# Filter stage of a four-layer graph network: a new order of DVE and PE work, four gather buffers, laps of four turns

## The reference, cut to what matters

```python
Wf = ssp(ssp(edge_attr @ m1_W + m1_b) @ m2_W + m2_b)     # 50 -> 256 -> 256, for each edge
msg = h1[src] * Wf                                       # 256 values for each edge
agg = jax.ops.segment_sum(msg, dst, num_segments=n_nodes)
# ssp(x) = softplus(x) - log(2)
```

## Time and profile before

| What | us |
|---|---|
| Median of the runs | 6121.58 |
| Runs, lowest to highest (3) | 6119.18 to 6132.07 |
| Span of the profiled execution, first to last instruction | 6128.0 |
| Filter stage in it, from the first instruction to the end of the last add | 4328.8 to 5264.5 |

### The profile page before, as it was taken

The page is one execution under the profiler, slowest core; times in us unless marked ns, Lnnn a source line. Parts: engine busy times, 40 slices in busy tenths (PEclk is TensorE's granted clock), DMA queues, the critical chain, the costliest instruction groups (busy, mean ns, idle before and its releaser), DMA issues. The chain is left out here.

```text
span 6128.0 us, 77751 instructions
## 1 busy us (share of the span) xinstructions
PE 4062.0 (66%) x17164; PEld 2958.9 (48%) x17165; DVE 3143.4 (51%) x7175; ACT 1987.0 (32%) x4687; POOL 3556.1 (58%) x2851
## 2 busy tenths in 40 slices
PE   5599922596777769677677444445688888745553
PEld 5488811353555555355556333333455555533332
DVE  5577636522555542355554344445477777533334
ACT  0122200000665541266563122220477777400000
POOL 0244411277777725677773788865555555478884
PEclk9999966798887879788787655557799999866555
DMA  0000002234665534566552233333234343243332
GB/s 7 24 10 10 10 27 61 77 77 94 172 168 154 158 89 92 135 171 166 153 156 61 62 84 83 84 79 89 71 102 103 103 104 103 79 101 84 84 84 73
DMA packets 511546, 558.56 MB, mean 91 GB/s; under 512 B 302820, under 2 KB 394959, under 8 KB 511005
## 3 DMA queue, kind: packets, MB, share of 16 engines
q0 software_dynamic: 349600, 362.07, 24.5%
q1 hardware_dynamic: 158408, 187.29, 10.7%
q10 hardware_dynamic: 3250, 6.40, 0.4%
HBM read 460.45 MB, written 92.22 MB: 90 GB/s over the span
## 5 line engine op out<-in xcount | busy, mean ns | idle before, releaser
L1259 POOL DMA_INDIRECT sum_gx_sb<-scratch_xw,keep_k_row_step_sb x1272 | 1602.7, 1260 | 469.9 <-issue 351.3
L1372 PE MATMUL sum_a_ps<-sum_gx_sb,sum_sel_sb 125*125 125x258 f32 (+1 forms) x4320 | 1214.4, 445 | 539.5 <-ACT sum_gx_sb L1308 218.9
L1372 PEld LDWEIGHTS sum_a_ps<-sum_gx_sb,sum_sel_sb 125*125 125x125 f32 x4320 | 936.1, 242 | 732.2 <-issue 514.1
L1308 ACT ACTIVATE sum_gx_sb<-sum_gx_sb,sum_wt_sb 125x129 f32<-125x129 f32 x3312 | 981.8, 388 | 561.5 <-DVE sum_wt_sb L1501 527.2
L2473 POOL DMA_INDIRECT filter_gx_sb<-scratch_h,keep_k_src_step_sb x424 | 513.5, 1211 | 410.6 <-DVEq L2620 299.0
L1168 POOL DMA_INDIRECT scratch_grouped<-keep_k_value_sb,keep_k_place_sb x400 | 481.7, 1204 | 272.6 <-issue 137.1
L2917 POOL DMA_INDIRECT source_gx_sb<-scratch_h,source_grouped_sb x424 | 527.5, 1244 | 140.4 <-issue 117.5
L2929 PE MATMUL source_s_ps<-source_gx_sb,source_sel_sb 125*125 125x257 f32 x848 | 370.0, 612 | 310.8 <-DMA source_gx_sb<-scratch_h,source_grouped_sb 310.8
L2929 PEld LDWEIGHTS source_s_ps<-source_gx_sb,source_sel_sb 125*125 125x125 f32 x848 | 246.3, 304 | 434.5 <-issue 172.1
L2527 PE MATMUL filter_ps<-filter_m_sb,filter_h_sb 128*125 128x256 f32 x1728 | 403.9, 387 | 15.6 <-DVE filter_f_sb L2592 15.3
L2527 PEld LDWEIGHTS filter_ps<-filter_m_sb,filter_h_sb 128*125 128x125 f32 x1728 | 318.2, 189 | 141.9 <-issue 98.2
(11 more groups left out here) (513 smaller groups left out, 6861.5 us busy)
## 6 DMA issues: line engine op xcount, KB each, us to landing
scratch_hots<-sum_cuts_sb SPq DMA_DIRECT2D x108, 244.1 KB
filter_sel_sb<-scratch_hots SPq DMA_DIRECT2D x106, 244.1 KB
sum_gx_sb<-scratch_xw,keep_k_row_step_sb POOLq DMA_INDIRECT x1272
scratch_xw<-gate_xsb_sb SPq DMA_DIRECT2D x50, 253.9 KB
scratch_xw<-attend_xsb_sb SPq DMA_DIRECT2D x25, 507.8 KB
filter_ea_sb<-in_ea_t SPq DMA_DIRECT2D x436, 24.4 KB
filter_gx_sb<-scratch_h,keep_k_src_step_sb POOLq DMA_INDIRECT x424
source_gx_sb<-scratch_h,source_grouped_sb POOLq DMA_INDIRECT x424
```

The source lines that it names most:

```text
L1259: nc.gpsimd.indirect_dma_start(out=gx[:, q, j, :], out_offset=None, in_=table, in_offset=bass.IndirectOffsetOnAxis(ap=keep["row_step"][:, ...
L1308: last = nc.scalar.activation(here, here, ACT.Copy, scale=wt[q][:, h, j:j + 1])
L1372: last = mm(psa[b][0:P, half, 0:BF], sel[:, 0, p, j, :], gx[:, q, at, half * BF:(half + 1) * BF], **flags)
```

## The change

- DVE's order in a turn becomes: `make_f2` for turn r+2, `make_h1` for r+3, `products` (the second softplus and the product) for r+1, then `add` for r. The messages `ms` get two buffers, so that they are made one turn ahead of the sums.
- PE's order becomes `hidden` for r+4, the sums for r, `filters` for r+3.
- `node_tiles` is called once a turn for four tiles, behind the product and ahead of the wait for the sums. The drain between product and `ms_made` is gone; the product raises `ms_made` itself, and POOL waits for `ms_made` in place of `used`.
- `gx` has four buffers with a semaphore each; POOL no longer waits for the weights at the start.
- The loops of all engines hold four turns (a lap) in place of two. Turns that don't exist are left out (`runs`), so the surplus `hidden` and `filters` are gone.
- The start: `ea_free` is raised before the clearing of `agg`, not after it.
- Each group's four adds, each with its drain, are kept as they are.

```diff
-    gx = mem.sb("gx", [P, 2, HF, D])
+    LAP = 4
+    QUADS = STEPS // HF
+    LOOPS = (QUADS - 6) // LAP
+    gx = mem.sb("gx", [P, LAP, HF, D])
...
-    f2, lg2 = ([mem.sb(f"{n}{q}", [P, HF, D]) for q in range(2)] for n in ("f2", "lg2"))
-    ms = mem.sb("ms", [P, HF, D])
+    f2, lg2, ms = ([mem.sb(f"{n}{q}", [P, HF, D]) for q in range(2)] for n in ("f2", "lg2", "ms"))
...
+    def laps(engine, lap):
+        lap(-1, LAP)
+        with engine.Fori(0, LOOPS) as i:
+            lap(i, LAP)
+        for i in range(LOOPS, -(-QUADS // LAP)):
+            lap(i, min(LAP, QUADS - i * LAP))
...
-            pool.wait_ge(landed, 16 * 4)
             for step in range(STEPS):
-                j, q = step % HF, step // HF % 2
-                if j == 0:
-                    pool.wait_ge(used, step // HF + 1)
+                j, n = step % HF, step // HF
+                if j == 0 and n >= LAP:
+                    pool.wait_ge(ms_made, n - LAP + 1)
...
+            def lap(i, count):
+                for r in range(count):
+                    load(i, r + 5)
+                    load_hots(i, r + 2)
...
+            def lap(i, count):
+                for r in range(count):
+                    hidden(i, r + 4)
+                    if runs(i, r):
+                        sums(i, r)
+                    filters(i, r + 3)
...
+            def lap(i, count):
+                for r in range(count):
+                    parts = []
+                    if runs(i, r + 1):
+                        act.wait_ge(f2_made, i * LAP + r + 2)
+                        parts.append(filters[(r + 1) % 2])
+                    if runs(i, r + 3):
+                        act.wait_ge(hid, i * LAP + r + 4)
+                        parts.append(hidden[(r + 3) % 2])
+                    log(parts)
...
+            def products(i, r):
+                if runs(i, r):
+                    dve.wait_ge(log2_made, i * LAP + r + 1)
+                    vec.scalar_tensor_tensor(f2[r % 2][:], f2[r % 2][:], 0.0, lg2[r % 2][:], ALU.max, ALU.add)
+                    dve.drain()
+                    dve.wait_ge(x_in[r % LAP], i * (16 * HF) + (r // LAP + 1) * (16 * HF))
+                    vec.tensor_tensor(ms[r % 2][:], f2[r % 2][:], gx[:, r % LAP], ALU.mult).then_inc(ms_made, 1)
+
+            def add(i, r, tiles):
+                dve.wait_ge(summed, i * LAP + r + 1)
+                for j in range(HF):
+                    here = agg[:, bass.ds(tiles[j], 1), 0:D].rearrange("p o f -> p (o f)")
+                    vec.tensor_tensor(here, ps3[0:P, j, :], here, ALU.add)
+                    dve.drain()
+                dve.nop().then_inc(added, 1)
+
+            def lap(i, count):
+                for r in range(count):
+                    make_f2(i, r + 2)
+                    make_h1(i, r + 3)
+                    products(i, r + 1)
+                    if runs(i, r):
+                        add(i, r, node_tiles(nc, keep, (i * LAP + r) * HF, HF))
+                    else:
+                        dve.drain()
...
             vec.memset(half[:], 0.5)
+            dve.drain()
+            dve.nop().then_inc(ea_free, 1)
             for t in range(0, NT + 1, 13):
                 vec.memset(agg[:, t:t + 13, 0:D], 0.0)
             dve.drain()
-            for sem in (ea_free, added, used, used):
-                dve.nop().then_inc(sem, 1)
+            dve.nop().then_inc(added, 1)
```

More of the change, by code:

```diff
@@ L2452, in filter_sum, with runs, later @@
     lg1, h1 = ([mem.sb(f"{n}{q}", [128, 2, C4]) for q in range(2)] for n in ("lg1", "h1"))
-    f2, lg2 = ([mem.sb(f"{n}{q}", [P, HF, D]) for q in range(2)] for n in ("f2", "lg2"))
-    ms = mem.sb("ms", [P, HF, D])
+    f2, lg2, ms = ([mem.sb(f"{n}{q}", [P, HF, D]) for q in range(2)] for n in ("f2", "lg2", "ms"))
     sel = mem.sb("sel", [P, 2, HF, P])
     ps1, ps2, ps3 = [mem.ps(f"1{q}", [128, 2, 512]) for q in range(2)], mem.ps("2", [128, HF, D]), mem.ps("3", [128, HF, D])
-    (landed, used, ea_free, hid, log1_made, h1_made, filt, f2_made, log2_made, ms_made,
+    (landed, ea_free, hid, log1_made, h1_made, filt, f2_made, log2_made, ms_made,
      summed, added) = (mem.sem(n) for n in (
-         "landed", "used", "ea_free", "hid", "log1_made", "h1_made", "filt",
-         "f2_made", "log2_made", "ms_made", "summed", "added"))
-    x_in, e_in, hot_in = ([mem.sem(f"{n}{q}") for q in range(2)] for n in ("x", "e", "hot"))
+         "landed", "ea_free", "hid", "log1_made", "h1_made", "filt", "f2_made", "log2_made", "ms_made",
+         "summed", "added"))
+    x_in = [mem.sem(f"x{q}") for q in range(LAP)]
+    e_in, hot_in = ([mem.sem(f"{n}{q}") for q in range(2)] for n in ("e", "hot"))
     vec, mm = nc.vector, nc.tensor.matmul
-    TURNS, U2 = STEPS // (2 * HF), 2 * HF
+    def runs(i, r):
+        return not isinstance(i, int) or 0 <= LAP * i + r < QUADS
+    def later(i, r, first):
+        return not isinstance(i, int) or LAP * i + r >= first
+    def laps(engine, lap):
[4 more added lines that the diff above has]
+            lap(i, min(LAP, QUADS - i * LAP))
     with nc.Block() as block:
@@ L2482, in _ @@
             sp.dma_start(mb[:], dr["L2_gnn_m2_b"].partition_broadcast(P)).then_inc(landed, 16)
[L2484 to L2491, removed]
@@ L2493, in _, with load @@
-            sp.wait_ge(ea_free, 1)
[L2494 to L2505, removed]
+            def load(i, r):
+                if runs(i, r):
+                    if later(i, r, 2):
+                        sp.wait_ge(hid, i * LAP + r - 1)
+                    for j in range(HF):
+                        tile = sp.value_load(keep["etile"][0:1, bass.ds((i * LAP + r) * HF + j, 1)], min_val=0, max_val=ET - 1)
+                        sp.dma_start(ea[0:50, r % 2, j, :], dr["ea_t"][:, bass.ds(tile * P, P)]).then_inc(e_in[r % 2], 16)
@@ new lines, in load_hots @@
+            def load_hots(i, r):
+                if runs(i, r):
+                    if later(i, r, 2):
+                        sp.wait_ge(summed, i * LAP + r - 1)
+                    sp.dma_start(sel[:, r % 2].rearrange("p j n -> p (j n)"), dr["hots"][:, bass.ds((i * LAP + r) * (HF * P), HF * P)]).then_inc(
+                        hot_in[r % 2], 16)
+            def lap(i, count):
+                for r in range(count):
+                    load(i, r + 5)
+                    load_hots(i, r + 2)
@@ L2506, in _ @@
+            sp.wait_ge(ea_free, 1)
+            load(-1, 4)
+            laps(sp, lap)
             for q in range(2):
-                sp.wait_ge(e_in[q], 16 * HF * (TURNS + 2 - q))
-                sp.wait_ge(hot_in[q], 16 * TURNS)
+                sp.wait_ge(e_in[q], 16 * HF * (QUADS // 2))
+                sp.wait_ge(hot_in[q], 16 * (QUADS // 2))
         @block.tensor
         def _(pe):
[L2512 to L2524, removed]
-                for j in range(HF):
-                    for b in range(2):
-                        last = mm(ps2[0:P, j, :], h1[q][:, b, j * P:j * P + P], m2[:, b, :], start=(b == 0), stop=(b == 1))
-                last.then_inc(filt, 1)
-            pe.wait_ge(landed, 16 * 4)
-            hidden(0, 0, 16 * HF)
-            hidden(1, 1, 16 * HF)
@@ L2533, in _, with hidden @@
[L2533 to L2546, removed]
+            def hidden(i, r):
+                if runs(i, r):
+                    pe.wait_ge(e_in[r % 2], i * (LAP // 2 * 16 * HF) + (r // 2 + 1) * (16 * HF))
+                    if later(i, r, 2):
+                        pe.wait_ge(h1_made, i * LAP + r - 1)
+                    for o in range(2):
+                        last = mm(ps1[r % 2][:, o, 0:C4], m1[0:51, 128 * o:128 * o + 128],
+                                  ea[0:51, r % 2].rearrange("p j e -> p (j e)"), start=True, stop=True)
+                    last.then_inc(hid, 1)
@@ new lines, in filters, with sums, ready @@
+            def filters(i, r):
+                if runs(i, r):
+                    pe.wait_ge(h1_made, i * LAP + r + 1)
+                    if later(i, r, 1):
+                        pe.wait_ge(f2_made, i * LAP + r)
+                    for j in range(HF):
+                        for b in range(2):
+                            last = mm(ps2[0:P, j, :], h1[r % 2][:, b, j * P:j * P + P], m2[:, b, :], start=(b == 0), stop=(b == 1))
+                    last.then_inc(filt, 1)
+            def sums(i, r):
+                def ready():
+                    pe.wait_ge(ms_made, i * LAP + r + 1)
+                    pe.wait_ge(added, i * LAP + r + 1)
+                    pe.wait_ge(hot_in[r % 2], i * (LAP // 2 * 16) + (r // 2 + 1) * 16)
+                ready()
+                for j in range(HF):
+                    last = mm(ps3[0:P, j, :], sel[:, r % 2, j, :], ms[r % 2][:, j, :], start=True, stop=True)
+                last.then_inc(summed, 1)
@@ L2548, in _ @@
+            def lap(i, count):
+                for r in range(count):
+                    hidden(i, r + 4)
+                    if runs(i, r):
+                        sums(i, r)
+                    filters(i, r + 3)
```

(23 more changed lines are left out.)

4 lines of the change are left out of this document (2 added, 2 removed).

## The result

| Kernel | Median us | Runs, lowest to highest | Ratio to before, 95% interval |
|---|---|---|---|
| before | 6120.38 | 6113.1 to 6132.07 (4) | |
| new | 6041.10 | 6037.21 to 6045.06 (4) | 0.987 [0.9856, 0.9884] |

The new kernel is 79 us faster, where 65 were forecast; 6041.1 lies inside the range of 6028 to 6100. The profiled execution has a span of 6035.4 us and took 6037.2.

What follows compares the result with a forecast made beforehand. A circle of waits bounds the old kernel; DVE would pace the new one at 7.93 us a turn. The stage's 59.4 us less, with the start 66, takes the median from 6121.6 to 6055 us, range 6028 to 6100.

Steps and rivals of the forecast that it cites:

- The bound: Filter stage, new order: DVE, not PE, sets the pace, at 7.93 us a turn against PE's 7.50.
- The load of four: DVE's register load of four node tiles behind the product: taken as 0.35 us, bounds 0.34 and 0.77.
- The pitch: Steady filter turns on DVE: 7.83 us plus 0.10 for the branch, 7.93 a turn against 8.43 before.
- The start: Start of the filter stage: ea_free raised earlier brings the first attribute load and first add 7.2 us forward.
- The end: Last two filter turns: 10.0 us for both, less 1.1 for the missing h1 of turn 103.
- The slack: Filter stage: the other engines have more than a microsecond to spare a turn, which hides the moved waits.
- PE-bound stage: Rival, filter stage: loads hide behind the product, DVE's turn 7.26 us under PE's 7.50; 6011 us, chance 0.05.
- The slower rival: DVE's longer filter loop stalls at each branch back, 24 x 4.1 = 98 us; 6153 us, chance 0.10.
- The third: Rival, filter stage: the circle of waits persists at 8.43 us a turn; 6115 to 6125 us, chance 0.05.

Runs made afterwards that it cites:

- e2: New kernel with two loads of two node tiles behind the product in place of one load of four: 6134.5 us, ratio to before 1.0006.
- e1: New kernel with the load of the four node tiles moved ahead of the products, behind make_h1: 5995.4 us, ratio to before 0.978.
- e6: New kernel with two gather buffers in place of four: 6048.4 us, ratio to before 0.9867.
- e5: New kernel with PE's old order inside a turn (hidden, filters, sums): 6560.8 us, one run.

## Why the prediction was right

- **The bound.** "DVE, not PE, would set the pace" was right. The trace shows it (no wait of DVE, waits of PE and ACT for DVE), and it holds under experiment in both directions: 0.8 us more of sequencer work gave 0.83 more a turn (e2), 0.64 less (1.79 to 1.15) gave 0.56 less, down to PE's own 7.25 (e1). PE waited 0.24 us a turn ahead of filters (22.9 us, 96 turns), where some 0.4 were forecast.
- **The load of four.** Taken at 0.35 us against a bound of 0.77; it was 345 ns. The figure of about 200 ns for each register, which the Trainium skill gives ("Runtime: NRT & Kernel Launch", "Instruction fetch mechanics"), doesn't hold for four values here: they cost less than two. How much hangs on this term, which the prediction called the uncertain one, e2 shows: with 0.8 us more behind the product the gain is gone.
- **The pitch** was 7.81 instead of 7.93. Means over the 90 turns from 4400 to 5100: f2 1.14, h1 1.11, L2620 to L2623 1.33 against 1.39, product to add 1.79 against 1.80, three adds 1.78, last add to f2 with the branch 0.66 against 0.61 + 0.10. So two terms were a little too long: the step that I had read at one row (1.39) and that is 1.28 or 1.29 in half of the turns, and the branch. The 103 turns took 802.0 us (4357.38 to 5159.36), where 816.8 less 1.1 were forecast: 13.7 less.
- **The start** gave 7.3 us (41.16 from the stage's start to the first add, 48.43 before) against 7.2.
- **The end** took longer: 12.5 us between the first adds of turns 103 and 105, where 10.0 were worked out. Rows of the new kernel, timeline of DVE:

```profile
5159.36 0.42 DVE L2629 TENSOR_TENSOR keep_agg_sb<-filter_ps,keep_agg_sb 125x256 f32 x1 [0.41 <-issue]
...
5165.59 0.42 DVE L2629 TENSOR_TENSOR keep_agg_sb<-filter_ps,keep_agg_sb 125x256 f32 x1 [1.38 <-PE filter_ps L2557]
...
5171.83 0.42 DVE L2629 TENSOR_TENSOR keep_agg_sb<-filter_ps,keep_agg_sb 125x256 f32 x1 [4.03 <-PE filter_ps L2557]
```

  Timeline of PE, same stretch:

```profile
5155.29 1.96 PE L2557 MATMUL filter_ps<-filter_ms_sb,filter_sel_sb 125*125 125x256 f32 x8 [1.41 <-issue]
5161.69 3.75 PE L2557 MATMUL filter_ps<-filter_ms_sb,filter_sel_sb 125*125 125x256 f32 x8 [4.44 <-issue]
5167.93 3.75 PE L2557 MATMUL filter_ps<-filter_ms_sb,filter_sel_sb 125*125 125x256 f32 x8 [2.49 <-issue]
```

  PE has nothing left but sums and stands idle between them; its granted clock is 1.00 from 5150 to 5160 and 0.50, which is 1.2 GHz, from 5165 to 5174. The last two groups of sums took 3.75 us each, where about 2.1 were counted, and DVE waits for both. The forecast took the clock to stay at 1.00 in the whole stage; two groups 1.65 us longer are more than the missing 2.5 us, since part of the first falls beside DVE's own work. In e6 the same two groups took 3.37 and 2.42 us, and the end 10.8. From the first add to that of turn 105 it took 814.5 us against 825.7 forecast: 13.7 less in the turns, 2.5 more at the end.
- **The slack** was judged right: DVE has no other wait in the steady part, and the four gather buffers were idle cover (e6).
- **The rivals.** The rate of a PE-bound stage was mis-sized: 7.50 us a turn was read off a timeline with waits in it, where a group of filters took 3.67 and one of sums 1.92 us; in e1, with every wait met in time, it is 3.55 and 1.83, and the turn 7.25. The slower rival was rightly held unlikely at about twice the instructions of the old loop: the stall exists from somewhere above 238 on. The third, that the circle persists, did not come about; with PE's old order another circle does, and a longer one (e5).

Not tried apart: the drain that was dropped behind the product, and the surplus `hidden` and `filters` that were left out.

## What to carry to other kernels

When every engine of a loop idles, write down for each the start-to-start time of its own instructions with the drains, register loads and branches of its sequencer; the largest sum, not the largest busy time, is what a reorder can reach. In this stage the register work left no gap when it stood behind two long instructions that were already issued (e1), and every part of it that reached past the product, ahead of the wait for the sums, came out in full (e2). So look first at where such loads stand: moving one line was worth 56 us here, and a like edit 1 us in an order where another wait ruled. Price one half of a reorder alone before trusting it: one half of this one made the kernel 433 us slower (e5, 6560.8 against 6127.6, one run). And where a change leaves PE with idle time between short groups, read the granted clock too: e5 and the stage's end took longer than was worked out, and in both it had fallen.

## What the runs showed of the hardware

- A register load's time doesn't simply grow with the number of values: on DVE one took 314 ns (L506, once in the trace before), two 525 to 529, three 766, and four only 340 to 358, in three different phases. What makes four cheap was not tried (their alignment or their number).
- Loops of DVE with 122 and 238 instructions branch back in 0.44 us more than a turn without branch; one of 473 has a gap of 4.28 us in the row above. The point between them was not measured. SP's loop of 252 has no such gap, its loop of 500 one of 5.0 us; PE's of 532 has none.
- With PE waiting 3 us in each turn (e5) its granted clock was 0.77 on average, and its filters took 5.2 to 6.5 us in place of 3.7: 12.8 us a turn in place of 10.5. At the end of the new kernel's stage, with 4.44 us of idle time between two groups, eight matmul records took 3.75 us at 0.50 in place of 1.96 at 1.00.
- When no wait is late (e1), a group of sums is followed by the next group 0.09 us sooner and one of filters 0.12 us sooner than in the timeline of before. Why was not looked into.
